# A first attention whose fill is laid out in another order: loads, context features, turned values and next keys

## The chip, the cores and the metric

The kernel runs on one core of a Trainium2 chip. The metric is the time of one execution on the device in microseconds (us), median of three runs; lower is better. The engines are TensorE (PE in the rows; its weight loads are PEld), VectorE (DVE), ScalarE (ACT), GpSimd (POOL) and SyncE (SP), which here only issues loads and stores.

## What is computed

Four layers, each a gated cross-attention and a gated feed-forward part, with x of 8 x 256 x 256 and a context ctx of 8 x 77 x 256 (float32). The change lies in the first attention. Cut to what matters:

```
z(v) = einsum('nshd,ed->nshe', v, fm_w) + fm_b        # 16 heads of 16
feature_map(v) = concat([exp(z), exp(-z)], -1)        # 32 a head
v, k, q = feature_map(ctx), feature_map(ctx), feature_map(layernorm(x))
attn = softmax(einsum('nqhd,nkhd->nhqk', q, k) / sqrt(256))
x = x + tanh(g_xattn[0]) * (einsum('nhql,nlhd->nqhd', attn, v) @ fc_w.T + fc_b)
# then: x + tanh(g_ffn[0]) * (layernorm(x) @ sign(W).T), a second attention with
# keys ctx @ Wk + bk, a ternary feed-forward, a top-64 attention, a mixture of
# eight experts, a third kind of attention, and a sign layer
```

Keys and values are the same features of the context: the keys are used as they lie (feature on the partition), the values are the same numbers turned by TensorE (key on the partition).

## The kernel before, in words

All engines run their own queue in order and are held together by semaphores (`wait_ge`); the order is written out by hand. `prep_p`, `prep_a`, `prep_v` count what TensorE, ACT and DVE have done of the context's preparation; `.past(n)` is n of them. Eight PSUM banks are shared by hand too.

**Loads** (`sync`, from L462): identity, context, four small constants, gates, rows, the feature weights `fmw`, `gb` (output biases), then x in one load of 2048 KB, then `fcw`, `sgw`, `w1q`, `w1k`, `w1v` and the weights of later layers.

**Fill.** TensorE (L2170 on) runs ten warming matmuls (`warm`), sixteen transposes of the context, eight more warming matmuls, then eight matmuls of 308 columns (L2185), which are the context features: four groups g of four heads by two halves of the batches, into banks 0 to 7. ACT copies the turned context to `ctxT` (L834) and takes the exp of the features into `kall` (L847). When all eight are done, TensorE turns the values of the eight batches (L2191, 32 transposes, banks in the order EMPTIED) and DVE copies each batch's out (L1397). DVE has the statistics of x's batches 0 and 1 (`lx_stats`, L1380, L1385) among them and then scales `gb` by the gates (L1401). POOL makes scale and shift from the statistics (`post_scale`, L565 to L573), ACT normalises (L852).

**First attention, loop over k** (TensorE L2300 on, ACT L904 on, DVE L1580 on, POOL L607 on). Batch b goes through: `lx_flip` (L2197, normalised x is turned), ACT copy (`lx_turned`), `lx_queries` (L2223), feature exp (`lx_features`, L875), `lx_keys` on POOL (L589), then four groups j: `lx_scores` (L2239, banks 4 and 5), DVE `lx_soft` (row maximum L1409, subtraction L1413), ACT `lx_exp` (L881), DVE `lx_total` (sum L1422, reciprocal L1425), POOL `lx_normal` (L602), `lx_flip_p` (L2256, banks 1 and 7), ACT copies, `lx_values` (L2266, bank 6), ACT copies; at the end `lx_final` (L2279) and DVE `lx_sum` (L1430). The scores of group i wait until DVE has emptied the two banks: `pe.wait_ge(sc_r[0].sem, sc_r[0].past(i))`. On TensorE, scores(b,3) stand in the iteration after scores(b,0) to (b,2), behind flip_p(b,0,0).

**Keys of the second attention** (`next_keys`, L2280 on): four pairs of 308-column matmuls into banks 6 and 7 (j = 0 to 3, bank 6 + j % 2), copied out by ACT (L899). Before, pair 0 and 1 stand in iteration 0 and pair 2 and 3 in iteration 1. flip_p(0,0,1) waits for all four.

## Time and profile before

| What | us |
|---|---|
| median of three runs | 914.85 (913.31 to 916.0) |
| the profiled execution, its own time | 918.2 |
| span of that execution in the trace | 916.4 |
| TensorE busy in the span | 805.4 (88%) |
| DVE busy in the span | 658.8 (72%) |
| ACT busy in the span | 496.1 (54%) |
| POOL busy in the span | 538.4 (59%) |

The span is from the first to the last instruction of the execution that the profiler recorded; its own time holds it and a little around it. A timeline row gives start, length, engine, line, operation, the tiles written and read by the program's names, how many instructions it merges, and in brackets the idle time before it with what ended it. In these rows `experts` is a large buffer in which many of the tiles named here live, `ps` is any PSUM bank. A matmul's end is modelled; a float32 matmul shows as two records, a transpose as one.

### The profile page before, as it was taken

Reading aid. Unit: us, or ns where it says so; the run is one execution under the profiler, and the core shown is the slowest. Engines: PE = TensorE matmul, PEld = TensorE weight load, DVE = VectorE, ACT = ScalarE, POOL = GpSimd, SP = SyncE. Lnnn points to the kernel's source line nnn. Section 1 sums busy time; section 2 is a strip of 40 time slices with the busy share of each in tenths; the row PEclk is TensorE's granted clock in tenths of the full one; section 3 lists DMA queues with packets and bytes.
Section 4 is the critical chain, followed back from the end, with each engine's and each line's share of the span. In section 5 each row is a group of like instructions: output and inputs, shape, how many; then the busy total and the mean of one; then the engine's idle time right before and its main releaser. Section 6 shows DMA issues by size and latency. Waiting matters only on the chain.

```text
span 916.4 us, 18952 instructions
## 1 busy us (share of the span) xinstructions
PE 805.4 (88%) x5836; PEld 633.7 (69%) x5842; DVE 658.8 (72%) x2767; ACT 496.1 (54%) x1272; POOL 538.4 (59%) x730
## 2 busy tenths in 40 slices
PE   6899998998787676777787689999999999998898
PEld 5677776886565444545566668888787879987775
DVE  2888786889978999999998473645564542425887
ACT  3877764668896777878777322111111111226673
POOL 2665644586652987888776214564556456237883
PEclk9999999999999697989999789999999999999999
DMA  9100001000000082000000562222222224140001
GB/s 292 58 1 2 2 1 46 1 1 1 1 1 1 2 338 77 1 25 24 9 18 30 169 212 80 36 41 37 42 42 44 35 54 92 22 104 1 13 32 51
DMA packets 37790, 46.70 MB, mean 51 GB/s; under 512 B 4294, under 2 KB 33838, under 8 KB 37691
## 3 DMA queue, kind: packets, MB, share of 16 engines
q1 hardware_dynamic: 29211, 35.77, 11.6%
q0 software_dynamic: 8480, 9.72, 6.9%
q8 instruction: 49, 0.80, 0.4%
q14 instruction: 50, 0.41, 0.1%
HBM read 33.80 MB, written 11.68 MB: 50 GB/s over the span
## 4 chain that ended last, share of the span: by engine, by line
PE 57%; DVE 25%; issue 6%; POOL 6%; ACT 5%; DMA 1%; DVEq 0%; ACTq 0%; POOLq 0%; SPq 0%
PE ps L2775 11%; PE ps L2786 11%; DVE experts L1646 5%; DVE experts L1632 4%; PE ps L2256 4%; PE ps L2279 3%; PE ps L2168 3%; DVE m8b L1639 3%; DVE m L1625 3%; PE ps L2239 2%; PE ps L2830 2%; PE ps L2804 2%; DVE mx L1622 2%; PE ps L2266 2%; PE ps L2197 2%
## 5 line engine op out<-in xcount | busy, mean ns | idle before, releaser
L1899 DVE COPY ptall<-experts 128x512 f32 x136 | 53.3, 434 | 94.8 <-PE ps L2775 64.8
L2775 PE MATMUL ps<-xnT,ptall 128*128 128x128 f32 x896 | 106.3, 278 | 0.0
L2775 PEld LDWEIGHTS ps<-xnT,ptall 128*128 128x128 f32 x896 | 104.0, 194 | 0.1
L2786 PE MATMUL ps<-experts,wk 128*128 x448 | 102.0, 381 | 1.4 <-ACT xkeep L1255 1.4
L1245 ACT ACTIVATE wk<-ps 128x1024 f32<-128x1024 f32 x34 | 34.8, 1025 | 113.6 <-PE ps L2775 93.5
L2786 PEld LDWEIGHTS ps<-experts,wk 128*128 128x128 f32 x448 | 82.9, 190 | 17.0 <-issue 6.8
L769 POOL DMA_INDIRECT xn<-expert_in,rown x34 | 34.5, 1016 | 91.1 <-PE ps L2763 59.2
L685 POOL TENSOR_TENSOR experts<-experts,mx 128x616 f32<-128x616 f32 x32 | 39.2, 1225 | 47.2 <-DVE experts L1646 47.0
L794 POOL DMA_INDIRECT token_sum<-xkeep,dest x28 | 47.6, 1701 | 31.9 <-ACT xkeep L1255 25.0
L602 POOL TENSOR_TENSOR experts<-experts,rden 128x616 f32<-128x616 f32 x32 | 38.8, 1217 | 44.5 <-DVE rden L1425 44.5
L1125 ACT ACTIVATE experts<-experts 128x77 f32<-128x77 f32 x256 | 64.1, 258 | 0.1
L1255 ACT ACTIVATE xkeep<-ps,ptall 128x256 f32<-128x256 f32 x34 | 16.1, 475 | 86.9 <-PE ps L2786 71.3
L2168 PE MATMUL ps<-ones 128*128 128x256 bf16 x434 | 57.2, 290 | 6.2 <-POOL mone L557 6.2
L2580 PE MATMUL ps<-ident,experts 128*77 128x128 f32 x256 | 36.5, 289 | 22.4 <-POOL experts L713 20.4
L1632 DVE MATCH_REPLACE8 experts<-m,experts 128x80 f32<-128x80 f32 x256 | 54.6, 230 | 0.0
L1646 DVE MATCH_REPLACE8 experts<-m8b,experts 128x80 f32<-128x80 f32 x256 | 54.6, 230 | 0.0
L2168 PEld LDWEIGHTS ps<-ones 128*128 128x128 bf16 x434 | 44.5, 104 | 14.5 <-ACTq L831 6.1
L710 POOL TENSOR_TENSOR rden<-ssum,mone 128x8 f32<-128x8 f32 x32 | 52.6, 1644 | 2.3 <-ACT experts L1125 2.3
L2591 PE MATMUL ps<-ptall,experts 77*32 77x256 f32 x256 | 22.7, 429 | 34.8 <-ACT ptall L1133 29.7
L834 ACT ACTIVATE ptall<-ps 77x512 f32<-77x512 f32 (+1 forms) x80 | 41.2, 546 | 21.4 <-PE ps L2256 18.2
L2580 PEld LDWEIGHTS ps<-ident,experts 128*77 128x77 f32 x256 | 31.0, 157 | 28.9 <-issue 28.1
L1125 ACT ACTIVATION_READ_ACCUMULATOR experts<-experts 128x1 f32 x256 | 49.3, 192 | 0.0
(359 smaller groups left out, 2363.7 us busy)
## 6 DMA issues: line engine op xcount, KB each, us to landing
experts<-in_ew SPq DMA_DIRECT2D x16, 1024.0 KB, 11.4
x<-in_x SPq DMA_DIRECT2D x1, 2048.0 KB, 10.9
xkeep<-in_bw SPq DMA_DIRECT2D x2, 1024.0 KB, 7.0
expert_in<-xkeep SPq DMA_DIRECT2D x8, 256.0 KB, 4.7
x<-token_sum SPq DMA_DIRECT2D x8, 256.0 KB, 3.7
out<-x SPq DMA_DIRECT2D x7, 256.0 KB, 2.1
token_sum<-x SPq DMA_DIRECT2D x4, 256.0 KB, 2.5
token_sum<-x SPq DMA_DIRECT2D x1, 1024.0 KB, 4.4
```

Of the source, the lines that this page charges most:

```text
L685: nc.gpsimd.tensor_tensor(dv, dv, mx[u][:, :].unsqueeze(2).broadcast_to([P, TB * HG, KEYS]), ALU.subtract).then_inc(sc_d.sem, 1)
L710: n = own_p.mark(nc.gpsimd.tensor_tensor(rden[u][:, :], ssum[u][:, :], mone[:, :], ALU.pow))
L794: gp.indirect_dma_start(acc_d, bass.IndirectOffsetOnAxis(ap=dest[:, at:at + 1], axis=0), ysb[u], None, compute_op=ALU.add).then_inc(s_st[u ...
L834: return nc.scalar.activation(dst, src, ACT.Copy)
L1125: ins = nc.scalar.activation(row, row, ACT.Exp, scale=-1.0, accum_out=ssum[u][:, j:j + 1])
L1632: ins = nc.vector.match_replace(d[j], m8[u][:, j, :], d[j], -BIG)
L1646: ins = nc.vector.match_replace(d[j], m8b[u][:, j, :], d[j], -BIG)
L1899: ins = nc.vector.tensor_copy(tilew[:, v, c, :], experts[:, bass.ds(e * EW + (c * FF + v * 512), 512)])
L2168: nc.tensor.matmul(bank(b)[:, 0:2 * P], hot[:, 0:P], hot, start=True, stop=True)
L2580: ins = nc.tensor.transpose(ps[2][0:KEYS, h // 2, at:at + P], pr[i % 2][:, t, h * KEYS:(h + 1) * KEYS], ident[:, :])
L2775: ins = nc.tensor.matmul(ps[j % 2][:, v, k * P:(k + 1) * P], tilew[:, v, c, k * P:(k + 1) * P], xTb[j % 3][:, c, :], start=c == 0, stop=c ...
L2786: ins = nc.tensor.matmul(bank(4)[:, 0:D], hidT[j % 2][:, k * P:(k + 1) * P], experts[:, bass.ds(e * EW + (E * EW + k * D), D)], start=k == ...
```

## The change

- x is loaded in three parts: batch 0 (256 KB), batch 1 (256 KB), the rest (1536 KB). `fmw` and `cols` come right behind the context, `lower` and `iota` far behind, `gb` and `rows` behind x. Waits follow: `s_x0`, `s_cst` (now three loads), `s_x`, and `s_fcw`, `s_w[1]`, `s_w[5]` with one or two loads more.
- The context is turned half by half, and TensorE's second row of eight warming matmuls is gone. Before the loop stand the features of half 0 (four) and the turned values of batches 0 to 2. Values of batch 3 and feature 4 are in iteration 0, features 5 to 7 and the values of batches 4 to 7 in iteration 1, in banks 1, 6 and 7 (FILL, TURNED).
- All four pairs of `next_keys` are in iteration 1: pair 0 before scores(0,2), pairs 1 to 3 behind queries(1). Pair 1 waits for DVE's seventh copy of values.
- ACT takes tanh of the gates in iteration 0. DVE copies the values of batches 4 and 5 behind lx_total(0,0), those of 6 and 7 behind lx_total(0,1), and scales `gb` behind lx_soft(0,0). POOL's lx_keys(0) waits for four exps, lx_keys(4) for eight.
- TensorE's waits for DVE copies in `lx_flip`, `lx_queries` and `lx_scores` of batch 0 go; a few later users (L1228, L1787, L2532) get a wait for `s_w[5]`.

```diff
@@ -413,7 +414,8 @@
         block = ctx.enter_context(nc.Block())
-        EMPTIED = (0, 2, 3, 6, 7, 4, 5, 1)
+        FILL = (4, 5, 6, 7, 6, 7, 1, 6)
+        TURNED = (1, 6, 7, 1, 7, 1, 7, 1)
@@ -461,13 +463,15 @@
             sp.dma_start(ctxn[:, :, :], a["ctx"].rearrange("b k d -> k b d")).then_inc(s_ctx, 16)
-            for dst, key in ((lower, "lower"), (iota, "iota"), (hsel, "hsel"), (cols, "cols")):
-                sp.dma_start(dst[:, :], a[key]).then_inc(s_cst, 16)
+            sp.dma_start(fmw[:, :, :], a["fmw"]).then_inc(s_w[0], 16)
+            sp.dma_start(cols[:, :], a["cols"]).then_inc(s_w[0], 16)
+            sp.dma_start(x[:, 0:TB, :], xv[:, 0:TB, :]).then_inc(s_x0, 16)
+            sp.dma_start(hsel[:, :], a["hsel"]).then_inc(s_cst, 16)
             sp.dma_start(graw[:, :], a["g"].partition_broadcast(P)).then_inc(s_cst, 16)
-            sp.dma_start(rows, a["rows"].partition_broadcast(KEYS)).then_inc(s_cst, 16)
-            sp.dma_start(fmw[:, :, :], a["fmw"]).then_inc(s_w[0], 16)
-            sp.dma_start(gb[:, :, :], a["outb"].partition_broadcast(P)).then_inc(s_w[0], 16)
-            sp.dma_start(x[:, :, :], xv).then_inc(s_x, 16)
+            sp.dma_start(x[:, TB:2 * TB, :], xv[:, TB:2 * TB, :]).then_inc(s_cst, 16)
+            sp.dma_start(x[:, 2 * TB:TT, :], xv[:, 2 * TB:TT, :]).then_inc(s_x, 16)
+            sp.dma_start(gb[:, :, :], a["outb"].partition_broadcast(P)).then_inc(s_fcw, 16)
+            sp.dma_start(rows, a["rows"].partition_broadcast(KEYS)).then_inc(s_w[1], 16)
             sp.dma_start(fcw[:, :, :], a["fcw"].rearrange("(c p) n -> p c n", p=P)).then_inc(s_fcw, 16)
@@ -479,6 +483,8 @@
             sp.dma_start(mrow8[:, :], a["mask"].partition_broadcast(P)).then_inc(s_w[4], 16)
+            for dst, key in ((lower, "lower"), (iota, "iota")):
+                sp.dma_start(dst[:, :], a[key]).then_inc(s_w[5], 16)
             sp.dma_start(rwT[:, :, :], a["rw"].rearrange("(c p) n -> p c n", p=P)).then_inc(s_w[5], 16)
@@ -580,8 +586,10 @@
                 if b == 0:
+                    gp.wait_ge(prep_a[0].sem, prep_a[0].past(4))
+                    gp.wait_ge(s_cst, 3 * 16)
+                if b == 4:
                     gp.wait_ge(prep_a[0].sem, prep_a[0].past(8))
-                    gp.wait_ge(s_cst, 6 * 16)
                 if b >= 2:
@@ -833,19 +841,21 @@
 
-            ac.wait_ge(s_cst, 6 * 16)
-            nc.scalar.activation(gates[:, :], graw[:, :], ACT.Tanh).then_inc(s_gate.sem, 1)
-            for c in range(CH):
-                for h in range(2):
-                    ac.wait_ge(s_ctp.sem, s_ctp.past(2 * c + h + 1))
+            for h in range(2):
+                for c in range(CH):
+                    ac.wait_ge(s_ctp.sem, s_ctp.past(2 * h + c + 1))
                     copy(ctxT[:, c, h * HALF:(h + 1) * HALF], bank(2 * c + h)[:, 0:HALF]).then_inc(s_cta.sem, 1)
...
 
-            ac.wait_ge(s_set.sem, s_set.past(3))
-            for j in range(2 * GR):
-                ac.wait_ge(prep_p[0].sem, prep_p[0].past(j + 1))
-                nc.scalar.activation(kall[:, j // 2, (j % 2) * HALF:(j % 2 + 1) * HALF], bank(j)[:, 0:HALF], ACT.Exp,
+            def ctx_features(n):
+                h, g = n // GR, n % GR
+                ac.wait_ge(prep_p[0].sem, prep_p[0].past(2 * GR * h + g + 1))
+                nc.scalar.activation(kall[:, g, h * HALF:(h + 1) * HALF], bank(FILL[n])[:, 0:HALF], ACT.Exp,
                                      bias=cols[:, 0:1]).then_inc(prep_a[0].sem, 1)
+
+            ac.wait_ge(s_set.sem, s_set.past(2))
+            for n in range(GR):
+                ctx_features(n)
@@ -909,7 +919,8 @@
                     lx_probs(k - 2, 2, 1)
                 if k == 1:
-                    next_keys(2)
+                    for n in range(GR + 1, 2 * GR):
+                        ctx_features(n)
                 if 0 <= k - 1 < B:
                     lx_exp(k - 1, 0)
@@ -917,13 +928,13 @@
                 if k < B:
                     lx_turned(k)
+                if k == 1:
+                    next_keys(0)
                 if 0 <= k - 2 < B:
                     lx_probs(k - 2, 3, 1)
...
                 if 0 <= k - 1 < B:
                     lx_exp(k - 1, 1)
-                if k == 1:
-                    next_keys(3)
                 if k < B:
                     lx_features(k, 0)
@@ -931,10 +942,17 @@
                     lx_features(k, 1)
                 if k == 0:
-                    next_keys(0)
+                    ac.wait_ge(s_cst, 3 * 16)
+                    nc.scalar.activation(gates[:, :], graw[:, :], ACT.Tanh).then_inc(s_gate.sem, 1)
+                    ctx_features(GR)
+                if k == 1:
                     next_keys(1)
                 if 0 <= k - 1 < B:
                     lx_exp(k - 1, 2)
+                if k == 1:
+                    next_keys(2)
+                    next_keys(3)
+                if 0 <= k - 1 < B:
                     lx_probs(k - 1, 0, 0)
                     lx_probs(k - 1, 0, 1)
@@ -1365,14 +1384,12 @@
 
-            ve.wait_ge(s_cst, 6 * 16)
             ve.wait_ge(s_w[0], 2 * 16)
-            ve.wait_ge(s_ctx, 2 * 16)
-            nc.vector.tensor_copy(identb[:, :], ident[:, :]).then_inc(s_set.sem, 1)
-
             neg = fmw[:, :, :].rearrange("p g (h s e) -> p (g h) s e", h=HG, s=2)[:, :, 1, :]
...
             nc.vector.tensor_tensor(cols[:, 0:1], cols[:, 0:1], cols[:, 15:16], ALU.mult).then_inc(s_set.sem, 1)
+            ve.wait_ge(s_ctx, 2 * 16)
+            nc.vector.tensor_copy(identb[:, :], ident[:, :]).then_inc(s_set.sem, 1)
@@ -1388,18 +1405,24 @@
 
-            ve.wait_ge(s_x, 16)
+            def ctx_values(b):
+                ve.wait_ge(prep_p[0].sem, prep_p[0].past(GR + 2 * GR * (b // GR) + b % GR + 1))
+                nc.vector.tensor_copy(v0[:, b, :, :], bank(TURNED[b])[0:KEYS, :].rearrange("p (h e) -> p h e", h=HEADS)
+                                      ).then_inc(prep_v[0].sem, 1)
+
+            def out_bias():
+                ve.wait_ge(s_gate.sem, s_gate.past(1))
+                ve.wait_ge(s_fcw, 2 * 16)
+                for k in range(2):
+                    nc.vector.tensor_scalar(gb[:, k, :], gb[:, k, :], gates[:, 2 * k:2 * k + 1], None, ALU.mult
+                                            ).then_inc(s_set.sem, 1)
+
+            ve.wait_ge(s_x0, 16)
             lx_stats(0)
-            for n, b in enumerate(EMPTIED):
-                if n == 4:
-                    lx_stats(1)
-                ve.wait_ge(prep_p[0].sem, prep_p[0].past(8 + n + 1))
-                nc.vector.tensor_copy(v0[:, b, :, :], bank(b)[0:KEYS, :].rearrange("p (h e) -> p h e", h=HEADS)
-                                      ).then_inc(prep_v[0].sem, 1)
-            ve.wait_ge(s_gate.sem, s_gate.past(1))
-            for k in range(2):
-                nc.vector.tensor_scalar(gb[:, k, :], gb[:, k, :], gates[:, 2 * k:2 * k + 1], None, ALU.mult
-                                        ).then_inc(s_set.sem, 1)
+            for b in range(GR):
+                ctx_values(b)
+            ve.wait_ge(s_cst, 3 * 16)
+            lx_stats(1)
@@ -1578,18 +1601,28 @@
 
             for k in range(B + 4):
+                if k == 2:
+                    ve.wait_ge(s_x, 16)
                 if 2 <= k < B:
                     lx_stats(k)
...
                     lx_soft(k - 3, 1)
                     lx_total(k - 3, 0)
+                    if k == 3:
+                        ctx_values(4)
+                        ctx_values(5)
                     lx_soft(k - 3, 2)
                     lx_total(k - 3, 1)
+                    if k == 3:
+                        ctx_values(6)
+                        ctx_values(7)
                     lx_soft(k - 3, 3)
                     lx_total(k - 3, 2)
...
                 if 0 <= k - 2 < B:
                     lx_soft(k - 2, 0)
+                if k == 2:
+                    out_bias()
                 if k - 4 == B - 1:
                     mid_stats_f(0)
@@ -2170,27 +2204,45 @@
             pe.wait_ge(s_ctx, 2 * 16)
-            for c in range(CH):
-                for h in range(2):
+            for h in range(2):
+                for c in range(CH):
                     for b in range(4):
...
 
-            warm(8, 7)
-            pe.wait_ge(s_cst, 6 * 16)
-            pe.wait_ge(s_cta.sem, s_cta.past(4))
-            pe.wait_ge(s_set.sem, s_set.past(3))
-            for j in range(2 * GR):
-                nc.tensor.matmul(bank(j)[:, 0:HALF], fmw[:, j // 2 % 2, :],
-                                 ctxT[:, j // 4, (j % 2) * HALF:(j % 2 + 1) * HALF],
+            def ctx_features(n):
+                h, g = n // GR, n % GR
+                if n < GR:
+                    pe.wait_ge(s_cta.sem, s_cta.past(g // 2 + 1))
+                elif n < 2 * GR - 1:
+                    pe.wait_ge(prep_v[0].sem, prep_v[0].past(n - GR + 2))
+                else:
+                    pe.wait_ge(prep_a[0].sem, prep_a[0].past(GR + 1))
+                nc.tensor.matmul(bank(FILL[n])[:, 0:HALF], fmw[:, g % 2, :], ctxT[:, g // 2, h * HALF:(h + 1) * HALF],
                                  start=True, stop=True).then_inc(prep_p[0].sem, 1)
-            pe.wait_ge(prep_a[0].sem, prep_a[0].past(8))
-            for b in EMPTIED:
+
+            def ctx_values(b):
+                if b == 0:
+                    pe.wait_ge(s_cta.sem, s_cta.past(4))
+                    pe.wait_ge(prep_a[0].sem, prep_a[0].past(GR))
+                elif b == 3:
+                    pe.wait_ge(prep_v[0].sem, prep_v[0].past(1))
+                elif b == 4:
+                    pe.wait_ge(prep_a[0].sem, prep_a[0].past(2 * GR))
+                elif b >= 6:
+                    pe.wait_ge(prep_v[0].sem, prep_v[0].past(b - 1))
                 for g in range(GR):
-                    ins = nc.tensor.transpose(bank(b)[0:KEYS, g * P:(g + 1) * P], kall[:, g, b * KEYS:(b + 1) * KEYS],
-                                              ident[:, :])
+                    ins = nc.tensor.transpose(bank(TURNED[b])[0:KEYS, g * P:(g + 1) * P],
+                                              kall[:, g, b * KEYS:(b + 1) * KEYS], ident[:, :])
                 ins.then_inc(prep_p[0].sem, 1)
+
+            pe.wait_ge(s_set.sem, s_set.past(2))
+            for n in range(GR):
+                ctx_features(n)
+            for b in range(GR - 1):
+                ctx_values(b)
+
             def flip(dst, src):
@@ -2284,9 +2330,9 @@
                     pe.wait_ge(s_w[2], 3 * 16)
-                    pe.wait_ge(prep_v[0].sem, prep_v[0].past(4))
+                    pe.wait_ge(prep_a[0].sem, prep_a[0].past(2 * GR))
                 elif j == 1 and part == 0:
-                    pe.wait_ge(prep_v[0].sem, prep_v[0].past(5))
+                    pe.wait_ge(prep_v[0].sem, prep_v[0].past(7))
                 elif part == 0:
@@ -2302,15 +2348,15 @@
                 if 0 <= k - 1 < B:
                     lx_scores(k - 1, 0)
+                if k == 1:
+                    for n in range(GR + 1, 2 * GR):
+                        ctx_features(n)
                 if 0 <= k - 2 < B:
                     lx_flip_p(k - 2, 1, 0)
...
                     lx_flip_p(k - 2, 2, 0)
                     lx_flip_p(k - 2, 2, 1)
-                if k == 1:
-                    next_keys(2, 0)
-                    next_keys(2, 1)
                 if 0 <= k - 1 < B:
                     lx_scores(k - 1, 1)
@@ -2319,21 +2365,28 @@
                     lx_flip(k)
                 if k == 0:
+                    ctx_values(GR - 1)
+                if k == 1:
+                    ctx_values(GR)
+                    ctx_values(GR + 1)
                     next_keys(0, 0)
+                    next_keys(0, 1)
                 if 0 <= k - 2 < B:
                     lx_flip_p(k - 2, 3, 1)
                     lx_values(k - 2, 2)
-                if k == 1:
-                    next_keys(3, 0)
-                    next_keys(3, 1)
                 if 0 <= k - 1 < B:
                     lx_scores(k - 1, 2)
...
                     lx_queries(k)
                 if k == 0:
-                    next_keys(0, 1)
-                    next_keys(1, 0)
-                    next_keys(1, 1)
+                    pe.wait_ge(s_set.sem, s_set.past(3))
+                    ctx_features(GR)
+                if k == 1:
+                    ctx_values(GR + 2)
+                    ctx_values(GR + 3)
+                    for j in range(1, 4):
+                        next_keys(j, 0)
+                        next_keys(j, 1)
                 if 0 <= k - 2 < B:
                     lx_values(k - 2, 3)
```

## Rows read from the trace of the kernel before

**Rows 1.** Stretches; columns: stretch and length in us, busy us of each engine, granted clock.
```profile
10.50:12.00 1.50, 1.50 (x9) 1.11 (x7) 0.00 (x0) 0.43 (x1) 0.00 (x0) 1.00 1.09 363
...
32.00:36.00 4.00, 2.60 (x24) 2.02 (x24) 3.72 (x7) 3.39 (x7) 1.33 (x2) 1.00 0.00 0
...
60.00:74.20 14.20, 14.20 (x126) 10.36 (x125) 11.51 (x22) 10.77 (x22) 8.67 (x11) 1.00 0.01 2
```

**Rows 2.** Chain of waits, 0 to 150 us; columns: start, length in us, what.
```profile
35.38 0.80 PE ps L2239 x8
```

**Rows 3.** Timeline, loads; start, length, engine, line; last row: issues, KB, us to landing.
```profile
5.26 0.43 SPq L470 DMA_DIRECT2D x<-in_x  x1
...
5.74 4.68 SPq L471 DMA_DIRECT2D experts<-in_fcw  x1
...
8.29 0.21 ACT L837 ACTIVATE gates<-graw 128x8 f32<-128x8 f32 x1 [1.19 <-DMA experts<-in_rows]
...
9.89 0.23 DVE L1371 CAST identb<-ident 128x128 bf16<-128x128 f32 x1 [9.89 <-DMA experts<-in_outb]
...
16.20 0.76 DVE L1380 BATCH_NORM_STATS2 st_e<-x 128x6 f32<-128x256 f32 x2 [5.88 <-DMA x<-in_x]
...
experts<-in_fcw SPq DMA_DIRECT2D x1, 512.0 KB, 11.9
```

**Rows 4.** Timeline, fill up to the feature exp, TensorE (PE), ACT, DVE.
```profile
6.17 2.29 PE L2168 MATMUL ps<-ones 128*128 128x256 bf16 x10 [6.17 <-POOL mone L557]
...
8.25 2.26 PE L2176 MATMUL ps<-ident,ctxn 77*128 77x77 f32 x16
...
9.01 1.97 ACT L834 ACTIVATE ctxT<-ps 128x308 f32<-128x308 f32 x4 [0.51 <-PE ps L2176]
...
10.31 1.91 PE L2168 MATMUL ps<-ones 128*128 128x256 bf16 x8
...
12.01 1.40 PE L2185 MATMUL ps<-ctxT,experts 128*128 128x308 f32 x4
...
13.00 4.08 ACT L847 ACTIVATE experts<-ps,cols 128x308 f32<-128x308 f32 x8 [2.02 <-PE ps L2185]
...
17.13 3.72 PE L2191 MATMUL ps<-ident,experts 128*77 128x128 f32 x32 [0.61 <-ACT experts L847]
...
17.83 2.48 DVE L1397 COPY experts<-ps 77x512 f32<-77x512 f32 x4 [0.66 <-PE ps L2191]
...
19.01 1.09 ACT L852 ACTIVATE experts<-x,nm_e,rs_e 128x256 f32<-128x256 f32 x2 [1.94 <-POOL nm_e L573]
...
20.69 0.60 PE L2197 MATMUL ps<-ident,experts 128*128 128x128 f32 x4
...
21.32 0.60 ACT L834 ACTIVATE experts<-ps 128x512 f32<-128x512 f32 x1 [1.22 <-PE ps L2197]
...
23.16 1.27 ACT L875 ACTIVATE wk<-ps,cols 128x512 f32<-128x512 f32 x2 [1.23 <-PE ps L2223]
```

**Rows 5.** Timeline, around the first scores.
```profile
23.04 1.82 PE L2292 MATMUL ps<-ctxT,experts 128*128 128x308 f32 x6
...
23.47 0.60 DVE L1401 TENSOR_SCALAR experts<-experts,gates 128x256 f32<-128x256 f32 x2
...
25.63 0.80 DVE L1409 TENSOR_REDUCE mx<-ps 128x8 f32<-128x616 f32 x1 [0.68 <-PE ps L2239]
...
28.24 0.80 DVE L1409 TENSOR_REDUCE mx<-ps 128x8 f32<-128x616 f32 x1
...
30.85 0.80 DVE L1409 TENSOR_REDUCE mx<-ps 128x8 f32<-128x616 f32 x1
...
32.17 0.66 PE L2256 MATMUL ps<-ident,experts 128*77 128x128 f32 x4 [0.49 <-POOL experts L602]
...
32.76 0.80 PE L2239 MATMUL ps<-experts,wk 64*128 64x154 f32 x8
...
33.60 0.80 DVE L1409 TENSOR_REDUCE mx<-ps 128x8 f32<-128x616 f32 x1 [0.17 <-PE ps L2239]
```

## What the change will do to the time: the prediction

> **What bounds the kernel now.** I read the table of stretches first, then the chain of waits, then the timeline of the first 36 us. Once the first attention runs, TensorE has no gap: it is busy 14.20 of the 14.20 us of one batch, DVE 11.51, ACT 10.77 [rows 1]. The chain of waits is TensorE without a break from 35.38 us on, when the scores of batch 1, group 0 start [rows 2]. Before that it is not: from 32 to 36 us TensorE works 2.60 of 4.00 us and DVE 3.72 [rows 1]. So whatever the new fill wins must still be there when that uninterrupted TensorE run starts. TensorE's order from scores(0,3) on (`lx_scores(0, 3)`: batch 0, group 3; 32.76 us) is the same in both kernels. I therefore compute two times: T0, when DVE starts on the first scores (25.63 us now), and the start of scores(0,3).
>
> **Part 1, the fill: T0 comes earlier.** Now: x lands at 16.20, statistics and scale take until the normalisation at 19.01 (2.81 us), and flip, copy, queries, feature exp, scores follow [rows 3, 4].
> Loads. Ahead of and with x's first part stand 1074 KB. The set before the first DVE operation was 1416 KB and had landed at 9.89 [rows 3], so the first part lands by 9.9. `fmw` and `cols` are in the first 818 KB; 1032 KB had landed at 8.29 [rows 3]. The scale and shift of batch 0 are ready by 9.9 + 2.8 = 12.7. x in three loads costs two more issues on SP's queue, 0.43 us each [rows 3], the second of them behind the first part; the two that were moved back (`lower`, `iota`) pay for them.
> Context features. The ctx transposes begin at 8.25 as before, and four of them take about 0.5 us. ACT copies at 9.01 and ends the four at 10.98 [rows 4]; half 0 is complete at about 9.95. The second row of eight warming matmuls (1.9 us from 10.31) is gone. The first feature matmul can start at 10.35, now 12.01; result to ACT 0.99 [rows 4]. With matmul and exp at 0.51 us each (eight exps in 4.08), four exps would end at 13.4.
> That is the price at TensorE's fast level, and the rows say otherwise for this stretch. The ten 256-column bf16 matmuls from 6.17 and the eight from 10.31 start 0.21 us apart, 256 columns at 1.2 GHz; the 77-column transposes start 0.128 apart and the later 128-column ones 0.109 [rows 4]. So TensorE ran at its lower level, though the granted clock is given as 1.00 from 10.5 to 12 us [rows 1], and rose to 2.4 GHz between 11.8 and about 12.5, after working without a pause since 6.17. The new features stand at 10.35, inside the slow stretch: at half speed a feature matmul is 1.03 us. If the rise comes at the same time, results reach ACT at about 11.7, 12.6, 13.15 and 13.65, and the exps end at 14.2. Bounds: 13.4 (fast at once) and 15.3 (slow throughout). I take 14.2, by the nearest row, the rise seen.
> From there, in the new order: normalisation of batch 0 on ACT 14.2 to 15.3 (1.09); beside it, twelve value transposes on TensorE, 14.2 to 15.5 (32 in 3.72); flip at 15.55, copy on ACT 0.63 after it at 16.15, the first feature exp 1.84 after the copy began (queries between) at 18.0, its first half (of 1.27) done at 18.65, scores at 18.75, DVE 0.84 later (32.76 to 33.60): **T0 = 19.6** [rows 4, 5]. The value transposes of batch 3 and ctx_features(4) fit TensorE's waits for ACT (16.0 to 16.8, 17.7 to 18.2). POOL's lx_keys(0), a single operation, waits for four exps instead of eight and starts at 14.2, 4.5 us before the scores want it. DVE needs four copies (0.62 each), stats(1) and stats(2) (about 1.0 each, 0.76 of it the first two operations [rows 3]): free by 19.4, no delay. stats(2) waits for the rest of x: 2877 KB against 3464 KB at 16.20 now, so before 16.2, needed at 18.4. Three matmuls of next_keys (from 23.04 on; a float32 matmul shows as two records) no longer stand before the first scores [rows 5].
> Gain at T0: 25.63 - 19.6 = **6.0 us**.
>
> **Part 2, from T0 to scores(0,3): given back.** Now this takes 32.76 - 25.63 = 7.13 us. DVE paces it: soft(0,0) at 25.63, soft(0,1) 28.24, soft(0,2) 30.85, 2.61 apart [rows 5].
> - `out_bias` behind soft(0,0): two operations in 0.60 [rows 5], less the 0.1 that DVE had to spare: +0.5. It waits for tanh (ACT, done before T0) and for fcw (5.74 + 11.9 = 17.6 now, with 3976 KB; 3799 KB in the new order [rows 3]), needed at 21.1.
> - ctx_values(4) and (5) on DVE behind total(0,0): 2 x 0.62 [rows 4] = +1.2, so soft(0,2) starts at T0 + 7.0 instead of T0 + 5.2.
> - Then comes what decides. TensorE's queue runs ctx_values(6), (7), next_keys(1), (2), (3), flip_p(0,0,0), scores(0,3). next_keys(1) writes bank 7, which holds the turned values of batch 6, so it waits for DVE's seventh copy (`prep_v` past 7). On DVE that copy stands behind soft(0,2) and total(0,1): 2.61 + 0.62. Behind it TensorE does six matmuls of 308 columns; three took 1.82 with the tail of the last, some 0.58 each, the exps suggest 0.51 [rows 4, 5]; I take 0.53, 3.2 us. Then flip_p(0,0,0), from 32.17 to the scores at 32.76, 0.59 [rows 5]. From soft(0,2) to scores(0,3): 2.6 + 0.6 + 0.05 + 3.2 + 0.6 = 7.05, now 32.76 - 30.85 = 1.9: +5.15. TensorE idles some 2.3 us in that wait, and DVE after copy (7) nearly 4.
> Sum of the loss: 0.5 + 1.2 + 5.15 = **6.9 us**; scores(0,3) starts at 19.6 + 14.0 = 33.6, soft(0,3) at 34.4 (now 33.60).
> ACT is no bound: with norm(1), exps 4 to 7 and next_keys(0) put before them, exp(0,0) still ends some 0.6 us before total(0,0) wants it and exp(0,1) 1.9 us before total(0,1); exp(0,2) is held behind next_keys(1), but DVE wants it only behind soft(0,3).
> At nothing: `lower` and `iota` later (used long after the first attention), `rows` and the extra waits on s_w (used behind the first attention), the three removed waits of TensorE, half-wise order of the ctx transposes. The three next_keys that were before T0 and the removed 1.9 us of warming are inside the two sums.
>
> **Sum.** 6.9 - 6.0 = +0.9 us. The profiled execution took 918.2 us around a span of 916.4; this makes 919.1 for it. The median of the three runs is 3.4 us lower (914.85), and a shift in the fill moves both alike: **915.7 us**. About 0.3%, 2.7 us, is what can be told from no change.
>
> **Rivals.**
> A. The wait for bank 7 does not end last (DVE is quicker, or the matmuls start beside it). TensorE would still have six matmuls before flip_p: free at T0 + 7.9, scores(0,3) at T0 + 11.7, 31.3 us: -1.5 us, 913.4, or 912.6 if the clock has risen by 10.35. The queue orders speak against it. 12%.
> B. The loop swallows the moved work: DVE and TensorE idle before 35 us, scores(0,3) still follows 7.1 us after T0. Then -6.0: 908.8. For it: TensorE has 1.4 us idle in 4 [rows 1]. Against it: it is the same 1.4 us that wait for a DVE busy 3.72, and the moved pieces need more. 6%.
> C, slower. TensorE stays at 1.2 GHz, because without eight matmuls it stands idle near 14 and 16 us. Features +1.1, value transposes +1.3, flip +0.45, queries +0.85, scores +0.8 over my sum (each as long again as in rows 4): T0 = 24.1, total +5.4: 920.3. It decides from T0 above 21.4. Against it: from 32 to 36 us TensorE works only two thirds of the time and its 128-column transposes do not lengthen [rows 1, 5]. 7%.
> The Trainium skill (TensorE: Matmul & The Clock Gate, Part 1: The HAM clock gate) says that the engine starts at its lower clock and that sustained activity releases it; by that rule taking warming work out may keep the low clock longer. The trace agrees with the start, 0.21 us for 256 columns, and shows no fall.
> D. The first part of x does not land early, since all loads share the queues: at 16.2, as now, normalisation would start at 19.0, T0 = 24.4, total +5.7: 920.6. Against it: 1416 KB had landed at 9.89. 3%.
>
> **Numbers.** My forecast 72%, nearly all of it within 0.3% (T0 from 18.8 to 20.7 gives +0.1 to +2.0; matmuls at 0.51 or 0.58 -0.1 or +0.3). A is mostly within 0.3% too. Faster: B and part of A, 9%. Slower: C, D and the upper edge, 12%. Same 79%. The range takes in A with 0.5 us to spare, the bounds of T0, and as much again for the scatter of the runs (913.31 to 916.0): 912.9 to 918.8; B, C and D lie outside.
>
> **What would show it.** Right: normalisation of batch 0 near 14.2, first DVE reduce on scores near 19.6, soft(0,2) near 26.6, TensorE idle some 2 us ahead of next_keys(1) with the releaser DVE copy, scores(0,3) near 33.6, the same 14.2 us a batch afterwards. Wrong: scores(0,3) before 31; an idle of DVE ahead of its statistics by a load; transposes at twice their length after 13 us; a batch that takes other than 14.2 us.

## The result and the profile after

The kernel with the change takes 917.45 us in the median of 20 runs (913.96 to 920.35), the kernel before in 20 runs beside them 916.1 us (913.14 to 917.21). The ratio is 1.0019, with a 95% interval of 1.0010 to 1.0028: 1.7 us slower (0.9 to 2.6), inside the 0.3% that was called no change. The forecast was +0.9 us, 915.7 for a median of 914.85.

Two markers tell the fill: **T0**, DVE's first maximum over scores, and the **stage end**, DVE's sum of the last batch of the first attention (`lx_sum(7)`; 144.52 us in the trace shown before). First the timeline of the kernel after, from the arrival of x's first part to T0 (start, length, engine, line, operation, tiles); it answers to [rows 3, 4].

```profile
7.75 0.75 DVE L1397 BATCH_NORM_STATS2 st_e<-x 128x6 f32<-128x256 f32 x2
...
8.69 1.97 ACT L842 ACTIVATE ctxT<-ps 128x308 f32<-128x308 f32 x4 [1.91 <-PE ps L2210]
...
9.98 3.17 PE L2222 MATMUL ps<-ctxT,experts 128*128 128x308 f32 x8
...
11.40 0.52 ACT L853 ACTIVATE experts<-ps,cols 128x308 f32<-128x308 f32 x1 [0.75 <-PE ps L2222]
...
12.15 1.55 ACT L853 ACTIVATE experts<-ps,cols 128x308 f32<-128x308 f32 x3 [0.23 <-PE ps L2222]
...
13.61 1.08 ACT L862 ACTIVATE experts<-x,nm_e,rs_e 128x256 f32<-128x256 f32 x2
...
13.85 1.50 PE L2236 MATMUL ps<-ident,experts 128*77 128x128 f32 x12 [0.70 <-ACT experts L853]
...
17.66 1.26 ACT L885 ACTIVATE wk<-ps,cols 128x512 f32<-128x512 f32 x2 [1.24 <-PE ps L2271]
...
19.25 0.80 DVE L1432 TENSOR_REDUCE mx<-ps 128x8 f32<-128x616 f32 x1 [0.51 <-PE ps L2285]
```

The first part of x is there at 7.75 us, the features start at 9.98, the four exps end at 13.7, the normalisation starts at 13.61 (19.01 before) and T0 is 19.25 (25.63 before). Then what came behind T0; it answers to [rows 5].

```profile
20.80 0.61 DVE L1417 TENSOR_SCALAR experts<-experts,gates 128x256 f32<-128x256 f32 x2
...
22.20 0.77 DVE L1432 TENSOR_REDUCE mx<-ps 128x8 f32<-128x616 f32 x1
...
24.65 1.23 DVE L1410 COPY experts<-ps 77x512 f32<-77x512 f32 x2
...
25.80 0.79 DVE L1432 TENSOR_REDUCE mx<-ps 128x8 f32<-128x616 f32 x1
...
28.28 1.23 DVE L1410 COPY experts<-ps 77x512 f32<-77x512 f32 x2
...
28.97 4.99 PE L2338 MATMUL ps<-ctxT,experts 128*128 128x308 f32 x12 [2.04 <-DVE experts L1410]
...
33.80 0.60 PE L2302 MATMUL ps<-ident,experts 128*77 128x128 f32 x4
...
34.33 0.80 PE L2285 MATMUL ps<-experts,wk 64*128 64x154 f32 x8
...
35.17 0.80 DVE L1432 TENSOR_REDUCE mx<-ps 128x8 f32<-128x616 f32 x1 [5.65 <-PE ps L2285]
```

DVE starts soft(0,1) at 22.20 and soft(0,2) at 25.80, with the two copies of 24.65 between them. TensorE stands idle for 2.04 us, released by a DVE copy (line L1410, `ctx_values`, of which the pair at 28.28 is batches 6 and 7), then works 4.99 us on twelve records (six matmuls of next_keys), and scores(0,3) start at 34.33; they were at 32.76 before. DVE has waited 5.65 us for them. The stretches of this trace (stretch and length, busy us of PE, PEld, DVE, ACT, POOL, granted clock, DMA share, GB/s) tell why 3.2 us became 5:

```profile
26.00:28.00 2.00, 0.93 (x8) 0.70 (x7) 1.97 (x3) 1.22 (x2) 0.03 (x1) 1.00 0.70 195
...
28.00:30.00 2.00, 1.03 (x2) 0.84 (x3) 1.48 (x4) 0.00 (x0) 1.22 (x1) 0.71 0.00 0
...
30.00:32.00 2.00, 2.00 (x5) 1.31 (x4) 0.00 (x0) 0.57 (x2) 0.00 (x0) 0.50 0.00 0
...
32.00:34.00 2.00, 2.00 (x9) 1.37 (x9) 0.00 (x0) 1.07 (x3) 0.00 (x0) 0.94 0.00 0
...
60.00:74.20 14.20, 14.20 (x129) 10.36 (x125) 11.52 (x22) 10.76 (x22) 8.66 (x10) 1.00 0.01 2
```

The granted clock is 0.50 from the end of the idle time to about 32 us, TensorE's level of 1.2 GHz (the trace's own clock record has it from 28.84 to 32.25). The batch later on takes the same 14.20 us as in [rows 1], without a gap. The last sum:

```profile
146.09 0.75 DVE L1453 SCALAR_TENSOR_TENSOR x<-ps,gates,x 128x512 f32<-128x512 f32 x1 [5.00 <-PE ps L2325]
```

So this trace has the stage end 1.57 us later than the one before (144.52). What lies behind the stage end does not show the change: from there to the end of the span it is 769.5 us here, 771.9 before, and 768.6 to 771.9 in six traces of the two kernels. That scatter of 3 us is larger than the shift, so the stage is compared below by its own times.

### The profile page after: what moved, and what is told of

It reads as the page before. It is cut to its first block, busy times and chain, and to the rows that moved or that the text cites. A ratio compares the mean times of both kernels' runs of the same rounds, so it can differ in the third digit from the quotient of the medians.

```text
span 915.6 us, 18946 instructions
## 1 busy us (share of the span) xinstructions
PE 807.6 (88%) x5834; PEld 632.8 (69%) x5834; DVE 657.8 (72%) x2767; ACT 495.4 (54%) x1272; POOL 535.2 (58%) x730
## 4 chain that ended last, share of the span: by engine, by line
PE 59%; DVE 21%; ACT 6%; issue 6%; POOL 6%; DMA 1%; DVEq 0%; ACTq 0%; POOLq 0%; SPq 0%
PE ps L2828 11%; PE ps L2839 11%; PE ps L2302 3%; DVE experts L1679 3%; DVE experts L1665 3%; PE ps L2325 3%; PE ps L2883 2%; PE ps L2857 2%; PE ps L2285 2%; DVE m L1658 2%; DVE m8b L1672 2%; PE ps L2202 2%; PE ps L2312 2%; PE ps L2613 2%; PE ps L2249 2%
## 5 line engine op out<-in xcount | busy, mean ns | idle before, releaser
L2202 PEld LDWEIGHTS ps<-ones 128*128 128x128 bf16 x426 | 44.6, 106 | 15.2 <-ACTq L839 5.8
```

What stands on the lines that cost most here:

```text
L2202: nc.tensor.matmul(bank(b)[:, 0:2 * P], hot[:, 0:P], hot, start=True, stop=True)
```

## Experiments

All times are in us and those of the profiled execution of each run; `T0 to end` is from T0 to the stage end and takes out what happened ahead of T0. "Again" is the same kernel, traced once more.

| run | first four features | T0 | end | T0 to end | next_keys, 12 records |
|---|---|---|---|---|---|
| before | - | 25.63 | 144.52 | 118.89 | - |
| before, again | - | 25.48 | 144.36 | 118.88 | - |
| before, batch 0 of x early | - | 25.34 | 144.22 | 118.88 | - |
| changed | 3.17 | 19.25 | 146.09 | 126.84 | 4.99 |
| changed, again 1 | 4.05 | 20.13 | 147.04 | 126.91 | 5.07 |
| changed, again 2 | 4.40 | 20.47 | 145.70 | 125.23 | 3.38 |
| changed, again 3 | 2.28 | 17.98 | 143.21 | 125.23 | 3.38 |
| warming back in the fill | 2.24 | 19.51 | 144.74 | 125.23 | 3.38 |
| x in one load | 2.28 | 23.38 | 148.61 | 125.23 | 3.38 |
| warming in the wait | 4.23 | 20.30 | 145.53 | 125.23 | 3.38 |
| copy of batch 6 earlier | 4.05 | 20.12 | 144.45 | 124.33 | 3.38 |
| scores(0,3) first | 2.28 | 18.57 | 142.73 | 124.16 | 3.38 |
| both | 4.40 | 20.47 | 143.96 | 123.49 | 3.38 |
| both, 20 matmuls more | 4.40 | 20.47 | 146.04 | 125.57 | 3.28 |

My theory was that T0 comes early as reckoned, and that TensorE's queue at the wait for bank 7 gives the gain back, with a fall of the clock on top; the rivals are named with each run. The pieces of code are cut: lines starting with + and - are the edit, `...` is what was left out.

**DVE's copy of batch 6 earlier.**
```diff
                     lx_soft(k - 3, 2)
+                    if k == 3:
+                        ctx_values(6)
                     lx_total(k - 3, 1)
                     if k == 3:
-                        ctx_values(6)
                         ctx_values(7)
```


> DVE copies the values of batch 6 between soft(0,2) and total(0,1), one sum and reciprocal (1.06 us) earlier. Theory (TensorE's queue stands at the wait for bank 7): next_keys(1) starts at 27.9 instead of 28.97, scores(0,3) at least 1.1 us earlier than 34.33; if the shorter idle (1.0 instead of 2.0 us) also keeps the clock at its upper level, 2.6 us earlier and the last sum of the stage at 143.5 instead of 146.09. Rival (the moved DVE work as such is the cost): the same work is still there, scores(0,3) stays at 34.3.

From the timeline of this run:

```profile
28.22 0.68 DVE L1410 COPY experts<-ps 77x512 f32<-77x512 f32 x1
...
28.95 3.38 PE L2339 MATMUL ps<-ctxT,experts 128*128 128x308 f32 x12 [1.13 <-DVE experts L1410]
...
32.70 0.80 PE L2286 MATMUL ps<-experts,wk 64*128 64x154 f32 x8
```

Measured from T0, next_keys(1) starts at 8.83 instead of 9.73, and the stage ends at T0 + 124.33 instead of 125.23: the 0.9 us by which the copy came earlier (1.06 expected) go through whole. The wait for bank 7 ends last, as the theory has it; the rival, under which nothing moves, is out. The absolute times of the expectation were missed because T0 was 20.12 here.

**Warming inside the wait.**
```diff
+                    warm(14, 0)
                     for j in range(1, 4):
                         next_keys(j, 0)
```


> Fourteen warming matmuls (1.5 us) into bank 0 ahead of next_keys(1), inside the wait of 2.0 us. Theory (the idle wait let the clock fall to 0.50, which stretched the six matmuls from 3.2 to 5.0 us): granted clock 1.00 from 26 to 34 us, scores(0,3) near 32.5, last sum of the stage 1.8 us earlier, near 144.3, kernel 1.8 us (0.2%) faster than with the change. Rival (the clock falls at that time for another reason, or the warming only delays): still 0.50 there, no gain or a loss up to 1.5 us.

The two TensorE rows of this run, from its timeline:

```profile
27.83 1.69 PE L2202 MATMUL ps<-ones 128*128 128x256 bf16 x14
...
30.02 3.38 PE L2338 MATMUL ps<-ctxT,experts 128*128 128x308 f32 x12 [0.50 <-DVE experts L1410]
```

The clock holds and next_keys takes 3.38 us. Over 10 runs the median is 915.54, equal to the kernel before in the runs beside it, ratio 1.0005 (0.9992 to 1.0018). The interval overlaps that of the change, so a gain is not shown by the times. The absolute times of the expectation were missed here too: T0 was 20.30, and the stage end 145.53 instead of 144.3. Nor is the cover shown by the trace: four of the six executions that have the full 2 us of idle time hold the clock through it (changed, again 2 and 3; warming back in the fill; x in one load).

**scores(0,3) ahead of next_keys(1).**
```diff
+                    lx_scores(k - 1, 3)
                     for j in range(1, 4):
                         next_keys(j, 0)
...
                 if 0 <= k - 2 < B:
-                    lx_scores(k - 2, 3)
+                    if k > 2:
+                        lx_scores(k - 2, 3)
```


> scores(0,3) stand ahead of next_keys(1) on TensorE, nothing else moves. Theory (place in the queue): scores(0,3) start at 27.5, soft(0,3) at 29.5 right behind DVE's copies, and scores(1,0) at 33.5 if the clock holds (35.3 if it falls) against 36.95; last sum of the stage at 142.7 (144.5) against 146.09, so 3.4 (1.6) us faster than the change and 1.8 us faster than the kernel before, or level with it. Rival (DVE's moved work is the cost): soft(0,3) still ends near 36.8, no gain.

TensorE in the timeline of this run:

```profile
26.89 0.79 PE L2285 MATMUL ps<-experts,wk 64*128 64x154 f32 x8 [0.64 <-DVE experts L1436]
...
28.29 3.38 PE L2338 MATMUL ps<-ctxT,experts 128*128 128x308 f32 x12 [0.60 <-DVE experts L1410]
...
32.37 0.63 PE L2302 MATMUL ps<-ident,experts 128*77 128x128 f32 x4 [0.26 <-ACT experts L909]
...
32.93 0.79 PE L2285 MATMUL ps<-experts,wk 64*128 64x154 f32 x8
...
35.84 1.07 PE L2302 MATMUL ps<-ident,experts 128*77 128x128 f32 x8 [0.52 <-ACT ptall L842]
```

scores(0,3) follow T0 by 8.32 us instead of 13.47, and DVE no longer waits for them. But scores(1,0) now stand behind six matmuls and two flips and start at T0 + 14.36, only 1.7 us earlier than with the change (T0 + 16.09), and 0.66 us of that is lost behind them, 0.52 of it in a wait for ACT ahead of 35.84. T0 to end falls by 1.07 us, not by 1.8. The stage end of 142.73 agrees with the expectation only because T0 was early. Median 914.05 over 10 runs, ratio to the kernel before 0.9994 (0.9980 to 1.0009). The rival, that DVE's moved work is the cost, falls in part: the order on TensorE was worth 1.1 us, and the rest lies elsewhere.

**Both, and both with more work.**

The earlier copy of batch 6 and scores(0,3) ahead of next_keys(1), together.

> Both mends: scores(0,3) ahead of next_keys(1), and DVE's copy of batch 6 between soft(0,2) and total(0,1). Times from T0, the first DVE reduce on scores: with the change 125.2 us to the last sum of the stage where the clock holds, 124.2 with the first mend alone. Theory (from T0 on TensorE is the bound, and only its idle can still be had): the 0.6 us of idle before next_keys(1) goes, T0 + 123.6, so 142.2 to 143.9 for a T0 of 18.6 to 20.3; 2 us (0.2%) faster than the change, 1 to 2 us faster than the kernel before. Rival (the rest of the loss is a wait on DVE or ACT, which the earlier copy adds to): T0 + 124.2 or more.

T0 + 123.49, as the theory had it; the idle time ahead of next_keys is gone. This is the best of the versions: 914.23 in the median of 12 runs, ratio 0.9991 (0.9976 to 1.0006), which can't be told from the kernel before. Then, on top of it:
```diff
                     lx_scores(k - 1, 3)
+                    warm(20, 0)
                     for j in range(1, 4):
```


> The kernel with both mends and twenty matmuls of 256 bf16 columns more (2.13 us at the upper clock) on TensorE between scores(0,3) and next_keys(1). Theory (with the waits mended, TensorE is the bound from T0 on, so any work put behind T0 costs its own length, as the features, value transposes and three next_keys that were moved there do): stage end at T0 + 123.5 + 2.1 = T0 + 125.6. Rival (DVE or ACT is the bound there and TensorE has room): T0 + 124.5 or less.

The added matmuls and next_keys in the timeline of this run:

```profile
29.52 2.36 PE L2203 MATMUL ps<-ones 128*128 128x256 bf16 x20
...
31.71 3.28 PE L2339 MATMUL ps<-ctxT,experts 128*128 128x308 f32 x12
```

Twenty matmuls take 2.19 us from start to start of the next, and T0 to end grows by 2.08 (123.49 to 125.57). With the waits mended TensorE is the bound at this place, and what is put there costs its own length. That the same holds for each piece that the change moved is argued from this and not tested piece by piece; the stretches give its sum. They run from T0 to the stage end (first of the busy times is TensorE's), for the second trace of the kernel before, the changed kernel where the clock held, and the kernel with both mends:

```profile
25.48:144.36 118.88, 114.69 (x982) 83.12 (x983) 93.08 (x163) 84.71 (x165) 66.46 (x76) 1.00 0.02 4
```

```profile
20.47:145.70 125.23, 120.20 (x1012) 87.46 (x1013) 95.71 (x169) 87.36 (x171) 68.91 (x79) 1.00 0.06 21
```

```profile
20.47:143.96 123.49, 120.28 (x1012) 87.48 (x1013) 95.74 (x169) 87.16 (x171) 68.89 (x79) 1.00 0.06 19
```

Before, TensorE has 982 records and 114.69 us of work behind T0 and idles 4.2 us. Changed, it has 1012 records: thirty more are the sixteen transposes of batches 4 to 7, three features and four matmuls of next_keys at two records each. They make 5.5 us of work, and the idle time grows from 4.2 to 5.0: together the 6.35 us between 118.88 and 125.23. The mends bring the idle time to 3.2, below that of the kernel before, and leave the 5.6 us of moved work: T0 to end is 4.6 us longer than before, against the 6.1 us won at T0 in the mean.

**x in one load.**
```diff
-            sp.dma_start(x[:, 0:TB, :], xv[:, 0:TB, :]).then_inc(s_x0, 16)
+            sp.dma_start(x[:, :, :], xv).then_inc(s_x0, 16)
...
-            sp.dma_start(x[:, TB:2 * TB, :], xv[:, TB:2 * TB, :]).then_inc(s_cst, 16)
-            sp.dma_start(x[:, 2 * TB:TT, :], xv[:, 2 * TB:TT, :]).then_inc(s_x, 16)
...
```
The waits for `s_cst` go from three loads to two, and the one for `s_x` goes.

> As changed, but x comes in one load of 2048 KB behind cols. Theory (the early first part of x is a condition of the early T0): x lands at about 14.3, normalisation of batch 0 at 17.1 instead of 13.6, T0 at 22.7 whatever the clock does before, stage end at T0 + 125.2 = 147.9, 3 us slower than the change. Rival (ACT's exps hold the normalisation anyway): T0 stays between 18.6 and 20.3.

From the timeline of this run, x's landing to T0:

```profile
13.90 0.75 DVE L1395 BATCH_NORM_STATS2 st_e<-x 128x6 f32<-128x256 f32 x2 [5.67 <-DMA x<-in_x]
...
16.71 1.09 ACT L860 ACTIVATE experts<-x,nm_e,rs_e 128x256 f32<-128x256 f32 x2 [4.44 <-POOL nm_e L577]
...
17.86 0.66 PE L2245 MATMUL ps<-ident,experts 128*128 128x128 f32 x4 [3.94 <-ACT experts L860]
...
19.21 2.08 PE L2267 MATMUL ps<-experts 64*128 64x256 f32 x8 [0.25 <-ACT experts L840]
...
23.38 0.80 DVE L1430 TENSOR_REDUCE mx<-ps 128x8 f32<-128x616 f32 x1 [1.97 <-PE ps L2281]
```

x lands at 13.90, the normalisation starts at 16.71, and TensorE idles 3.94 us. T0 is 23.38, 0.7 later than reckoned: the clock fell behind the 3.94 us of idle time (granted 0.50 from 19.07 to 22.48 us), and the queries take 2.08 us against 1.13 in the run with both mends. The early part of x is a condition of the early T0.

**The same in the kernel before.**
```diff
+            sp.dma_start(x[:, 0:TB, :], xv[:, 0:TB, :]).then_inc(s_x0, 16)
             for dst, key in ((lower, "lower"), (iota, "iota"), (hsel, "hsel"), (cols, "cols")):
...
-            sp.dma_start(x[:, :, :], xv).then_inc(s_x, 16)
+            sp.dma_start(x[:, TB:TT, :], xv[:, TB:TT, :]).then_inc(s_x, 16)
...
```
The wait for `s_x` stands ahead of the statistics of batch 1.

> The kernel before with batch 0 of x loaded by itself right behind the context, nothing else. Theory (there the flip of batch 0 waits behind 32 value transposes on TensorE, not for x): the normalisation runs at 17.1, T0 stays at 25.6 and the stage end at 144.5. Rival (x's landing at 16.2 holds T0): T0 up to 1.9 us earlier.

From the timeline of this run, normalisation, flip and the first next_keys matmul:

```profile
16.26 1.08 ACT L854 ACTIVATE experts<-x,nm_e,rs_e 128x256 f32<-128x256 f32 x2
...
19.97 0.60 PE L2200 MATMUL ps<-ident,experts 128*128 128x128 f32 x4
...
20.96 0.79 PE L2295 MATMUL ps<-ctxT,experts 128*128 128x308 f32 x2 [0.39 <-DMA experts<-in_w1v]
```

The normalisation is 2.75 us earlier (16.26 against 19.01), the flip behind 32 value transposes 0.7 us earlier (19.97), and then TensorE waits for the weights of next_keys; T0 to end is unchanged and T0 is 25.34, 0.14 under the second trace of the kernel before. So x did not hold T0 there, which the rival had. The early x alone is worth next to nothing, the new order with x at 13.90 gives 2.2 us (23.38 against 25.56 in the mean of the two traces before), and both together 6.1.

**The warming back, and how far the clock moves.**
```diff
+            warm(8, 7)
             pe.wait_ge(s_set.sem, s_set.past(2))
             for n in range(GR):
                 ctx_features(n)
```


> The eight removed warming matmuls are back between the context's transposes and its first features, the rest as changed. Theory (cover of nothing in the new order, features run at 1.2 GHz until the clock rises at about 12): features start at 11.7 instead of 9.98, run at the upper level, the four exps end at 14.8 instead of 13.7, first DVE reduce 1.1 us later, at 20.3, stage end 147.2. Rival (the warming buys an earlier or steadier clock): first reduce at 19.3 or before, and the fall at 29 us gone.

Warming, features and next_keys in the timeline of this run:

```profile
9.98 1.36 PE L2202 MATMUL ps<-ones 128*128 128x256 bf16 x8
...
11.18 2.24 PE L2222 MATMUL ps<-ctxT,experts 128*128 128x308 f32 x8
...
29.23 3.38 PE L2339 MATMUL ps<-ctxT,experts 128*128 128x308 f32 x12 [2.03 <-DVE experts L1410]
```

The features start 1.2 us later and take 2.24 us; eight matmuls of warming took 1.36 us where 1.9 was seen before, so the clock rose during them (the trace's clock record begins at 10.63 us). T0 is 19.51: later than in two traces of the new order with a rise by 10.1 (17.98 and 18.57), earlier than in those with a rise from 13.5 on (20.12 to 20.47). And the same 2.03 us of idle passed without a fall. One trace does not tell theory from rival here, so both kernels were traced again.

> The kernel before once more, to see how far the clock's rise moves between executions: its features start at 12.0 behind 18 warming matmuls. Theory (TensorE's clock rises anywhere from 10 to 14 us in different executions; in the new order the first four features stand in that stretch, in the old one they are covered): T0 between 25.4 and 26.3 and T0 + 118.9 to the stage end. Rival (the new order causes the spread of T0 in some other way): T0 at 25.6 within 0.1, with the clock rising at 12.2 as in the first trace.

> The changed kernel once more, first of three looks at what the clock does. Theory (the moment at which TensorE's clock rises moves from execution to execution, and the 2.0 us wait before next_keys(1) lets it fall in some executions and not in others): T0 between 18.5 and 20.5 by whether the four first features take 2.3 to 4.3 us on TensorE; the last sum of the stage at T0 + 125.2 with the six matmuls of next_keys in 3.4 us, at T0 + 126.8 with them in 5.0 us. Rival (fall and rise belong to the program): features 3.17 us and the fall at 29 us each time, as in the first trace.

> Second look at the changed kernel. As for the first: by the theory one of the two lengths of next_keys, 3.4 or 5.0 us, and T0 from 18.5 to 20.5; by the rival always 5.0 us and T0 at 19.25.

> Third look at the changed kernel. As for the first: by the theory one of the two lengths of next_keys, 3.4 or 5.0 us, and T0 from 18.5 to 20.5; by the rival always 5.0 us and T0 at 19.25.

The four features and next_keys in the timelines of the three further traces of the changed kernel, one after the other:

```profile
9.98 4.05 PE L2222 MATMUL ps<-ctxT,experts 128*128 128x308 f32 x8
...
29.85 5.07 PE L2338 MATMUL ps<-ctxT,experts 128*128 128x308 f32 x12 [2.04 <-DVE experts L1410]
```

```profile
9.98 4.40 PE L2222 MATMUL ps<-ctxT,experts 128*128 128x308 f32 x8
...
30.20 3.38 PE L2338 MATMUL ps<-ctxT,experts 128*128 128x308 f32 x12 [2.04 <-DVE experts L1410]
```

```profile
9.60 2.28 PE L2222 MATMUL ps<-ctxT,experts 128*128 128x308 f32 x8
...
27.70 3.38 PE L2338 MATMUL ps<-ctxT,experts 128*128 128x308 f32 x12 [2.03 <-DVE experts L1410]
```

The same program needs 4.05, 4.40 and 2.28 us for its first features (3.17 in the trace above), by when the clock rises, and T0 is 20.13, 20.47 and 17.98. The same wait of 2.04 us is followed by the lower level in two of four executions. So fall and rise do not belong to the program, as the rival had it. The kernel before has T0 at 25.63 and 25.48; the second fits its theory (25.4 to 26.3) and misses its rival (25.6 within 0.1) by 0.02 us, too little to decide. The stage end spreads over 3.8 us in the changed kernel and 0.16 in the two traces of the one before. But in those two the clock rose at 12.40 and 11.72 us; what a rise at 14 does to the old order was not seen, so that the old order is the steadier one is not shown by the traces. The mean of the changed kernel's four is 145.51, 1.1 us above the 144.44 of the two; the times over 20 runs say 1.7 (0.9 to 2.6), and their spread is wider too, 6.4 us against 4.1.

## Why the prediction was right

- **T0.** 19.6 forecast, 19.25 measured, 19.46 in the mean of four traces; the gain of 6.0 us is 6.1. Flip, copy, queries and scores followed as reckoned. The step "I take 14.2, by the nearest row" (end of the four exps) was 13.7 here and moves from 12.4 to 14.9 with the clock's rise; my bounds for it, 13.4 and 15.3, were drawn around one execution and missed the early side, as did "T0 from 18.8 to 20.7" (17.98 was seen). And Part 1 has flip follow x and the normalisation in the old fill; there the 32 value transposes held it too, and an early x alone gave 0.14 us.
- **Up to soft(0,2).** "soft(0,2) starts at T0 + 7.0": measured T0 + 6.55. soft(0,1) starts at T0 + 2.95, so `out_bias` cost 0.34 and not 0.5, and the rest of the difference is in the copies and the overlap of DVE's starts (3.60 from soft(0,1) to soft(0,2), 3.8 by my terms).
- **The wait for bank 7.** The mechanism is as put: 2.04 us of idle (2.3 forecast), the releaser a DVE copy, scores(0,3) at T0 + 13.47 where the clock holds (14.0 forecast), and the earlier copy moved it by its own amount. The loss by then is 6.3 us, not 6.9. But "what decides", the words for this wait, is too strong: of the 6.35 us from T0 to the stage end 5.5 are moved work and 0.84 is more idle time, and both mends of the order together get 1.74 back.
- **The sum.** 6.3 - 6.1 = +0.2 where the clock holds; the +0.9 was too high in its loss. What is missing to the measured 1.7 is the step I left out: "3.2 us" for the six matmuls holds at the upper level only. In two of four executions they take 5.0, +1.6 us each time. Half of 1.6 over +0.2 is +1.0 to the stage end, near the 1.1 of the four traces. So it is luck that +0.9 lies so near: 0.6 us too much in the loss and 0.8 us of clock that I put at nothing nearly cancel. The last 0.6 us to the measured 1.7 are inside its interval (0.9 to 2.6) and have no cause shown.
- **Rival C** named the right resource at the wrong place. I expected the low clock in the fill, with 5.4 us, and set against it that in the trace before "its 128-column transposes do not lengthen". They don't, there; the change itself makes the pause in which the clock falls, behind T0. In the fill the low clock was not kept, it only ended at another time in each execution. The Trainium skill (TensorE: Matmul & The Clock Gate, Part 1: The HAM clock gate) says that the point of the rise differs from run to run, by half a microsecond either way, and that idle time brings the lower clock back. The traces agree with both in kind, with two falls in four, but not in size: the rise lies between 9.18 and 14.94 us, and the features are from 2.28 to 4.40 us long.
- **Rival A** is excluded by the earlier copy, **B** by scores(0,3) at T0 + 13.47 and not 7.1, **D** by x at 7.75 us. D's price at T0, 4.8 us, was reckoned too low: with x in one load T0 came 9.48 us behind x's landing at 13.90, so a landing at 16.2 would put it near 25.7, 6.2 us later than 19.46 (an estimate from these rows; the fall of the clock in that trace is in it).

What stays open: whether fourteen warming matmuls really guard the wait. One trace with the clock held is no proof, where it holds in four of six without them. Open too is what makes the clock fall behind the same wait in one execution and not in another.

## What to carry to other kernels

An earlier first result is worth little when the work that was taken out of its way comes to stand on an engine that is full afterwards. Here 6 us were won ahead of T0 and 5.5 us of TensorE work came to stand behind it, where TensorE had idled only 4.2 us in 119, and a wait was added. When work is moved into a loop, write down for each piece what stands behind it in its queue, and who frees its buffer: one copy in the wrong place on DVE held six matmuls, and they held the scores. And reckon with the level of TensorE's clock in the first 15 us and behind each new pause; take more than one trace.

## What the runs showed of the hardware that was not expected

- TensorE starts work at 5.84 us in all four executions of the changed kernel, without a pause until the features are done, and yet its clock rises at very different times: the trace's clock record begins, at the upper level, at 9.18 us in one of them (features of 2.28 us from 9.60), at 11.77 and 13.55 in two and at 14.94 in the fourth (4.40 us from 9.98). Ahead of its first entry the trace has no clock record at all, and the stretches print 1.00 for it; there only the lengths of the records show the lower level.
- A later fall, on the other hand, is in the granted clock: 0.50 for about 3 us. After the same idle time of 2.03 to 2.04 us it came in two of six executions. In those two the idle time began 15.2 and 14.3 us behind the rise (11.77 to 26.93, 13.55 to 27.82), in three others 13.2, 16.5 and 16.6 us behind it; in the sixth, which had fallen and risen once already, 8.6 us. Whether the fall hangs on this distance was not tested.
